# Dense stage of a split-float32 FFN: row tiles in pairs, 896 of 1160 columns by seven block products in place of eight

## The reference, cut to what matters

```
W = weights[condition]                        # one 64x64 matrix per batch, 16 in all
z = einsum('bct,bcd->bdt', x, W)              # mixes the 64 channels of a batch
result = einsum('bnd,od->bno', z, W_base) + b_base
probs  = softmax(einsum('bnd,ed->bne', z, W_gate))          # 8 experts
top_p, top_i = top_k(probs, 2); top_p /= sum(top_p)
h = einsum('bnd,erd->bner', z, A)             # 8 experts of rank 16
out = x + result + einsum('bner,eor->bno', h * route_w, B)
```

## Time and profile before

| | |
|---|---|
| median of 3 runs | 1025.07 us (1024.55 to 1025.69) |
| span of the profiled execution, first to last instruction | 1023.8 us |
| TensorE (PE) busy | 1015.4 us, 5834 matmuls |
| VectorE busy | 372.2 us |
| ScalarE busy | 209.5 us |
| GpSimd busy | 339.2 us |
| DMA | 107.09 MB, mean 105 GB/s |

### The profile page before, as it was taken

The page is one execution under the profiler, slowest core; times in us unless marked ns, Lnnn a source line. Parts: engine busy times, 40 slices in busy tenths (PEclk is TensorE's granted clock), DMA queues, the critical chain, the costliest instruction groups (busy, mean ns, idle before and its releaser), DMA issues.

```text
span 1023.8 us, 17244 instructions
## 1 busy us (share of the span) xinstructions
PE 1015.4 (99%) x5834; PEld 1007.7 (98%) x5834; DVE 372.2 (36%) x1240; ACT 209.5 (20%) x470; POOL 339.2 (33%) x264
## 2 busy tenths in 40 slices
PE   8999999999999999999999999999999999999998
PEld 6999999999999999999999999999999999999998
DVE  6533333333333333333333333333333333333334
ACT  6211211211122112111221221112212212122121
POOL 1424334233243342432423424324234243242331
PEclk9999999999999999999999999999999999999999
DMA  9323132232231322322213223223132232222311
GB/s 306 147 104 119 68 121 95 90 123 82 102 122 62 123 91 94 123 82 102 112 73 123 88 96 123 82 102 115 69 123 86 99 123 82 102 105 79 123 66 57
DMA packets 32009, 107.09 MB, mean 105 GB/s; under 512 B 3457, under 2 KB 6914, under 8 KB 32002
## 3 DMA queue, kind: packets, MB, share of 16 engines
q1 hardware_dynamic: 32000, 107.00, 28.5%
q10 hardware_dynamic: 2, 0.00, 0.0%
HBM read 73.43 MB, written 33.55 MB: 105 GB/s over the span
## 4 chain that ended last, share of the span: by engine, by line
PE 97%; DVE 1%; DMA 1%; SPq 1%; ACT 0%; issue 0%; DVEq 0%
PE ps_z L521 77%; PE ps_out L533 10%; PE ps_out L548 9%; DMA table_raw<-in_cond_w 1%; PE ps_hwt L541 1%; SPq L221 1%; DVE w_lo L421 0%; DVE w L462 0%; SPq L224 0%; DVE z_lo L431 0%; DVE table L484 0%; ACT table L376 0%; DVE o_sb L444 0%; SPq L234 0%; DVE pick L466 0%
## 5 line engine op out<-in xcount | busy, mean ns | idle before, releaser
L521 PE MATMUL ps_z<-w_hi,x_hi 128*128 128x384 f32 (+1 forms) x1536 | 526.0, 342 | 1.5 <-DVE w_lo L421 1.4
L521 PE MATMUL ps_z<-w_hi,x_lo 128*128 128x384 f32 (+1 forms) x1536 | 519.7, 338 | 0.0
L521 PE MATMUL ps_z<-w_lo,x_hi 128*128 128x384 f32 (+1 forms) x1536 | 519.5, 338 | 0.0
L306 POOL TENSOR_TENSOR x_lo<-xt_sb,x_hi 128x1024 fp32r<-128x1024 f32 x62 | 149.2, 2407 | 550.7 <-ACT x_hi L353 550.7
L521 PEld LDWEIGHTS ps_z<-w_hi,x_hi 128*128 128x128 f32 x1536 | 288.5, 188 | 5.7 <-DVE w_lo L421 1.9
L521 PEld LDWEIGHTS ps_z<-w_lo,x_hi 128*128 128x128 f32 x1536 | 288.7, 188 | 0.0
L521 PEld LDWEIGHTS ps_z<-w_hi,x_lo 128*128 128x128 f32 x1536 | 288.7, 188 | 0.0
L431 DVE TENSOR_TENSOR z_lo<-ps_z,z_hi 128x384 fp32r<-128x384 f32 (+1 forms) x192 | 107.6, 560 | 485.6 <-ACT z_hi L357 485.6
L357 ACT CAST z_hi<-ps_z 128x384 fp32r<-128x384 f32 (+1 forms) x192 | 92.4, 481 | 613.2 <-PE ps_z L521 612.3
L311 POOL TENSOR_TENSOR o_sb<-o_sb,bias 128x1024 f32<-128x1024 f32 x64 | 153.4, 2397 | 2.0 <-DMA o_sb<-in_x 2.0
L533 PE MATMUL ps_out<-z_hi,mix 128*128 128x384 f32 (+1 forms) x384 | 129.6, 337 | 1.1 <-POOL mix L299 0.8
(11 more groups left out here) (41 smaller groups left out, 362.0 us busy)
## 6 DMA issues: line engine op xcount, KB each, us to landing
o_sb<-in_x SPq DMA_DIRECT2D x64, 512.0 KB, 3.3
out_x<-o_sb SPq DMA_DIRECT2D x63, 512.0 KB, 2.6
xt_sb<-in_x_t SPq DMA_DIRECT2D x62, 512.0 KB, 4.4
w_raw<-in_w_t SPq DMA_DIRECT2D x8, 384.0 KB, 9.0
w_raw<-in_w_t SPq DMA_DIRECT2D x8, 196.0 KB, 4.9
xt_sb<-in_x_t SPq DMA_DIRECT2D x4, 256.0 KB, 4.8
table_raw<-in_cond_w SPq DMA_DIRECT2D x2, 256.0 KB, 8.7
b_raw<-in_b_t SPq DMA_DIRECT2D x1, 512.0 KB, 11.8
```

Source lines behind the costliest of these rows:

```text
L306: pool.tensor_tensor(x_lo[slot][:], xt_sb[slot][:], x_hi[slot][:].bitcast(F32), ALU.subtract).then_inc(s_x_lo, 1)
L521: mm = pe.matmul(z_bank(i, c)[:, 0:width[c]], a[slot][:, k, :], w[:, k, cols(c)], start=(k == 0 and q == 0), stop=(k == KT - 1 and q == 2))
```

## The change

Row tiles are worked in pairs (tile 2p is t = 0, tile 2p+1 is t = 1). The weight columns are cut anew: L is 312 base columns with the 136 of A and the gate (448), Q is 448 base columns, R is 264 base columns. Over L and Q the pair is a 2x2 block product: the rows are the two tiles, the inner axis has two halves of 4 blocks k, the columns are L and Q. It is done by Strassen's seven products in Winograd's form (`strassen`, 12 matmuls of 448 columns each) in place of eight, R stays plain (`plain_r`, 12 matmuls of 264 columns each, four times). Four blocks of x (`A11`, `A12`, `A21`, `A22`, 512 elements in a partition) are loaded into `raw`; four sums of them, S1 to S4, are made on GpSimd, four sums of weights, T1 to T4, once on VectorE. S4 is written in place over `raw[A12]`, the lo part of S1, S2 and S3 in place over the sum. The products accumulate in the banks `ps_1`, `ps_6` and `ps_5`: `u2` = P1 + P6, `u3` = u2 + P7, and VectorE's `add` brings a copy of P1 and earlier sums together out of them. The first pair is plain, while the weights arrive and T1 to T4 are made. The stores of the last pair go out in six parts.

How many instructions of each kind a pair has, before and after, is this:

| per pair | before | after |
|---|---|---|
| dense matmuls | 144 (48 of 392, 96 of 384 columns) | 132 (84 of 448, 48 of 264) |
| mix matmuls | 18 | 18 (12 of 448, 6 of 264) |
| lora matmuls | 18 | 18 (6 each of 312, 448, 264) |
| transposes | 2 | 2 |
| GpSimd passes over 512 elements | 0 | 12 (4 blocks' lo, 4 sums, 4 sums' lo) |
| GpSimd passes over 1024 elements | 4 | 2 |
| ScalarE passes over 512 elements | 0 | 8 (and none of the 2 over 1024) |
| VectorE adds of banks | 0 | 5 |

The diff, cut to the loop of each engine:

```diff
-BASE_COLS = [256, 384, 384]
+BASE_COLS = [312, 448, 264]
...
+            def load_raw(p, j):
+                tile, half = 2 * p + j // 2, j % 2
+                src = x_t[tile] if isinstance(tile, int) else \
+                    x_t[bass.ds(tile, 1)].rearrange("a p k r -> (a p) k r")
+                sp.dma_start(raw[j][:], src[:, half * KH:(half + 1) * KH, :]).then_inc(s_raw_in[j], 16)
...
+            def store(p, t):
+                sp.wait_ge(s_out[t][(Q, R)[t]], p + 1)
+                sp.dma_start(out[bass.ds((2 * p + t) * P, P), :], o_sb[t][:]).then_inc(s_stored[t], 16)
...
+            def step(p, last):
+                sp.wait_ge(s_stored[0], 16 * p)
+                load_x(p, 0)
+                if not last:
+                    sp.wait_ge(s_a_lo[A21], p + 1)
+                    load_raw(p + 1, A21)
+                    sp.wait_ge(s_a_lo[A22], p + 1)
+                    load_raw(p + 1, A22)
+                    sp.wait_ge(s_s_sum[3], p)
+                    load_raw(p + 1, A11)
+                    sp.wait_ge(s_s_lo[4], p)
+                    load_raw(p + 1, A12)
+                store(p - 1, 1)
+                sp.wait_ge(s_stored[1], 16 * p)
+                load_x(p, 1)
+                if not last:
+                    store(p, 0)
+            pairs(sp, step)
...
+            def sum_s1(p):
+                pool.wait_ge(s_raw_in[A21], 16 * p + 16)
+                pool.wait_ge(s_raw_in[A22], 16 * p + 16)
+                pool.wait_ge(s_p[5], p)
+                pool.tensor_tensor(s1[:], raw[A21][:], raw[A22][:], ALU.add).then_inc(s_s_sum[1], 1)
+            def sum_s2(p):
+                pool.wait_ge(s_s_sum[1], p)
+                pool.wait_ge(s_p[3], p)
+                pool.tensor_tensor(s2[:], s1[:], raw[A11][:],
+                                   ALU.subtract).then_inc(s_s_sum[2], 1)
+            def sum_s3(p):
+                pool.wait_ge(s_p[7], p)
+                pool.tensor_tensor(s3[:], raw[A11][:], raw[A21][:], ALU.subtract).then_inc(s_s_sum[3], 1)
+            def sum_s4(p):
+                pool.wait_ge(s_s_sum[2], p)
+                pool.wait_ge(s_a_lo[A12], p + 1)
+                pool.tensor_tensor(raw[A12][:], raw[A12][:], s2[:], ALU.subtract).then_inc(s_s_sum[4], 1)
...
+            def step(p, last):
+                sum_s2(p)
+                a_rest(p, A12)
+                sum_s4(p)
+                s_rest(p, 2, s2[:], s2_hi, s2_lo)
+                sum_s3(p)
+                s_rest(p, 3, s3[:], s3_hi, s3_lo)
+                s_rest(p, 1, s1[:], s1_hi, s1_lo)
+                a_rest(p, A22)
+                a_rest(p, A21)
+                pool.wait_ge(s_mixed[0][Q], p)
+                fetch_mix(p, 0)
+                pool.wait_ge(s_mixed[1][R], p)
+                fetch_mix(p, 1)
+                s_rest(p, 4, raw[A12][:], s2_hi, s2_lo)
+                residual(p, 0)
+                if not last:
+                    a_rest(p + 1, A11)
+                residual(p, 1)
+                if not last:
+                    sum_s1(p + 1)
...
+            def s_top(p, j, whole, hi):
+                act.wait_ge(s_s_sum[j], p)
+                act.copy(hi[:], whole).then_inc(s_s_hi[j], 1)
...
+            def added_top(p, t, c):
+                act.wait_ge(s_z_sum[t, c], p)
+                z_top(t, c, z_sum[t][:, cols(c)])
...
+            def step(p, last):
+                act.wait_ge(s_p[1], p + 1)
+                act.copy(z_sum[1][:, cols(L)], ps_1[:, 0:NS]).then_inc(s_p1_out, 1)
+                hwt_top(2 * p - 1)
+                act.wait_ge(s_p[6], p + 1)
+                s_top(p, 4, raw[A12][:], s2_hi)
+                act.wait_ge(s_p[2], p + 1)
+                z_top(0, L, ps_1[:, 0:NS])
+                s_top(p, 1, s1[:], s1_hi)
+                act.wait_ge(s_r_sum[0], p + 1)
+                z_top(0, R, ps_r[:, 0:width[R]])
+                if not last:
+                    a_top(p + 1, A11)
+                    a_top(p + 1, A12)
+                exps(2 * p)
+                added_top(p, 1, Q)
+                added_top(p, 1, L)
+                hwt_top(2 * p)
+                added_top(p, 0, Q)
+                if not last:
+                    s_top(p + 1, 2, s2[:], s2_hi)
+                exps(2 * p + 1)
+                act.wait_ge(s_r_sum[1], p + 1)
+                z_top(1, R, ps_r[:, 0:width[R]])
+                if not last:
+                    a_top(p + 1, A21)
+                    a_top(p + 1, A22)
+                    s_top(p + 1, 3, s3[:], s3_hi)
...
+            def added_rest(p, t, c):
+                z_rest(p, t, c, z_sum[t][:, cols(c)])
+            def add(bank, other, to):
+                return dve.tensor_tensor(to, bank[:, 0:NS], other, ALU.add)
...
+            def step(p, last):
+                dve.wait_ge(s_p1_out, p)
+                dve.wait_ge(s_p[6], p + 1)
+                add(ps_6, p1, u2).then_inc(s_u2, 1)
+                hwt_rest(2 * p - 1)
+                output(p - 1, 1, L)
+                z_rest(p, 0, L, ps_1[:, 0:NS])
+                output(p - 1, 1, Q)
+                output(p - 1, 1, R)
+                z_rest(p, 0, R, ps_r[:, 0:width[R]])
+                gate(p, 0)
+                dve.wait_ge(s_p[7], p + 1)
+                add(ps_6, p1, u3).then_inc(s_u3, 1)
+                dve.wait_ge(s_p[5], p + 1)
+                dve.wait_ge(s_u3, p)
+                add(ps_5, u3, u3).then_inc(s_z_sum[1, Q], 1)
+                added_rest(p, 1, Q)
+                dve.wait_ge(s_p[4], p + 1)
+                add(ps_6, p1, p1).then_inc(s_z_sum[1, L], 1)
+                hwt_rest(2 * p)
+                added_rest(p, 1, L)
+                dve.wait_ge(s_p[3], p + 1)
+                dve.wait_ge(s_u2, p)
+                add(ps_5, u2, u2).then_inc(s_z_sum[0, Q], 1)
+                output(p, 0, L)
+                added_rest(p, 0, Q)
+                output(p, 0, R)
+                gate(p, 1)
+                z_rest(p, 1, R, ps_r[:, 0:width[R]])
+                output(p, 0, Q)
...
+            def product(bank, hi, lo, u_hi, u_lo, opens, closes, goes_on=False):
+                for k in range(KH):
+                    for q, (a, w) in enumerate(((hi, u_hi), (hi, u_lo), (lo, u_hi))):
+                        mm = pe.matmul(bank[:, 0:w.shape[-1]], a[:, k, :], w[:, k, :],
+                                       start=(opens and k == 0 and q == 0),
+                                       stop=(closes and k == KH - 1 and q == 2), skip_group_check=goes_on)
+                return mm
+            def strassen(bank, hi, lo, g, opens):
+                return product(bank, hi, lo, w_hi[:, g], w_lo[:, g], opens, True, goes_on=not opens)
...
+            def step(p, last):
+                pe.wait_ge(s_a_lo[A11], p + 1)
+                strassen(ps_1, a_hi[A11], a_lo[A11], B11, True).then_inc(s_p[1], 1)
+                pe.wait_ge(s_out[0][Q], p)
+                mix_chunk(p - 1, 1, Q)
+                pe.wait_ge(s_out[0][R], p)
+                mix_chunk(p - 1, 1, R)
+                pe.wait_ge(s_t_lo[2], 1)
+                pe.wait_ge(s_s_lo[2], p)
+                strassen(ps_6, s2_hi, s2_lo, T2, True).then_inc(s_p[6], 1)
+                turn_hw(2 * p - 1)
+                pe.wait_ge(s_p1_out, p)
+                pe.wait_ge(s_a_lo[A12], p + 1)
+                strassen(ps_1, a_hi[A12], a_lo[A12], B21, False).then_inc(s_p[2], 1)
+                pe.wait_ge(s_hwt_lo, 2 * p)
+                lora(1, L)
+                lora(1, Q)
+                lora(1, R)
+                plain_r(ps_r, 0, 0, True, False)
+                plain_r(ps_r, 0, 1, False, True).then_inc(s_r_sum[0], 1)
+                pe.wait_ge(s_out[1][L], p)
+                mix_chunk(p, 0, L)
+                pe.wait_ge(s_t_lo[3], 1)
+                pe.wait_ge(s_s_lo[3], p)
+                pe.wait_ge(s_u2, p)
+                strassen(ps_6, s3_hi, s3_lo, T3, False).then_inc(s_p[7], 1)
+                pe.wait_ge(s_t_lo[1], 1)
+                pe.wait_ge(s_s_lo[1], p)
+                strassen(ps_5, s1_hi, s1_lo, T1, True).then_inc(s_p[5], 1)
+                pe.wait_ge(s_out[1][R], p)
+                mix_chunk(p, 0, R)
+                pe.wait_ge(s_t_lo[4], 1)
+                pe.wait_ge(s_a_lo[A22], p + 1)
+                pe.wait_ge(s_u3, p)
+                strassen(ps_6, a_hi[A22], a_lo[A22], NT4, False).then_inc(s_p[4], 1)
+                turn_hw(2 * p)
+                pe.wait_ge(s_s_lo[4], p)
+                pe.wait_ge(s_z_sum[1, Q], p)
+                strassen(ps_5, s2_hi, s2_lo, B22, False).then_inc(s_p[3], 1)
+                pe.wait_ge(s_hwt_lo, 2 * p + 1)
+                lora(0, L)
+                lora(0, R)
+                pe.wait_ge(s_a_lo[A21], p + 1)
+                plain_r(ps_r, 1, 0, True, False)
+                pe.wait_ge(s_out[0][L], p + 1)
+                mix_chunk(p, 1, L)
+                plain_r(ps_r, 1, 1, False, True).then_inc(s_r_sum[1], 1)
+                pe.wait_ge(s_out[1][Q], p)
+                mix_chunk(p, 0, Q)
```

(49 more changed lines are left out.)

603 lines of the change are left out of this document (300 added, 303 removed).

## The result

The changed kernel took 1206.05 us, the median of four runs (1205.79 to 1211.13), against 1024.84 us, the median of four, for the kernel before on the same chip: a ratio of 1.1778, 95% interval 1.1757 to 1.1799. The forecast was 1185 us, slower; the range 1045 to 1295. The profiled execution was the slowest of the four, 1211.13 us; its span of 1209.0 us lies 2.95 us above the median.

What follows compares the result with a forecast made beforehand. TensorE, 99% busy, was taken to bound the kernel before; afterwards a ring of in-order waits. 15.8 + 31.5 + 30 x 36.5 + 34.0 + 8 = 1184.3 of span, plus 1.3 for the median: 1185 us, range 1045 to 1295.

Steps and rivals of the forecast that it cites:

- Step 2: GpSimd's list from S1's lo to S4's lo at 10.2 us; first mix fetch ends at 7.1, TensorE idle 2.8 us.
- Step 5: TensorE from P4 round to the next P2: five products 12.2 us, the rest 6.7, together 18.9 us.
- rival D: TensorE's clock halves after the 3.65 us idle, doubling P4: 2.4 us a pair, 1257 us; after both idles 1330; chance 0.13.
- the forecast's signs: Expected in the profile: 170 matmuls a pair, TensorE some 80% busy, period 36.5 us, P4 and mix waits, clock 1.00.
- Contention, 1.0 on the path: VectorE's remainders and gates meet GpSimd passes and each engine waits for the other: 1.0 us a pair, bounds 0 and 4.
- rival C: VectorE-GpSimd contention decides if A12 lands at 4.8 us, gates running into passes: 4 us more a pair, 1305 us; chance 0.11.
- Rival B: A12-to-exponential link absent or covered, only mix late on TensorE: 31.8 us a pair, 1045 us; chance 0.08.
- the link through A12: A12's load after S4's lo, then ScalarE's cast ahead of the exponential, delays gate, u3 and P4: TensorE idle 3.65 us.
- the late reload of x: x for residual(p,1) lands at 17 us; S2's lo ends about 26, P6 wants S2 at 30.5, so hidden.
- the first ring: From P2 through GpSimd, A12's load, ScalarE and gate to P4, then TensorE back to P2: 16.6 + 18.9 = 35.5 us.
- Rival A: All waits hidden, TensorE's work alone counts: 29.0 us a pair, 956 us in total; chance 0.07.
- The ends: Opening and last pair outside the loop: opening 5 us above its 31.5 of matmuls, last pair 34.0, bare tail 3 more.

Runs made afterwards that it cites:

- the best order: Changed kernel with GpSimd's list filled, mix Q and R behind P6 and the exponential ahead of the casts: 970.59 us, ratio 0.9478 to the kernel before.

## Why the prediction was right, point by point

The direction, the mechanism and its place held; the total was 21 us (1.8%) low. That it came so near is partly luck, since two errors of a pair nearly cancelled. By its steps, counted from the end of P2 at 509.32:

| step | forecast | measured |
|---|---|---|
| TensorE's pace, 448 / 264 columns | 0.203 / 0.121 | 0.205 / 0.122 |
| GpSimd pass over 512 | 1.22 | 1.24 from start to start (511.89 to 514.36 for two) |
| S1's lo begins | 1.4 | 1.33 |
| mix ready, TensorE idle | 7.1, 2.8 | 5.94, 1.6 |
| S4's lo ends | 10.2 | 9.03 |
| load of A12 | 3.0 | 2.98 (518.50 to about 521.5) |
| exponential to hw | 2.04 | 2.03 |
| P4 starts, TensorE idle | 16.6, 3.65 | 15.42, 3.5 |
| P4 to the end of P2 | 18.9 + 1.0 | 21.67 |
| period | 36.5 | 37.09 here, 37.08 mean |
| ends | 89.3 | 1209.0 - 1112.4 = 96.6 |

**Step 2, the fetch**, was too dear by 1.2 us. The forecast carried over 0.90 us ahead of the first cast from the earlier trace rows; in the new list the cast at 514.36 follows A21's lo with no gap. The likely reason is that the register load is read while the passes before it run, where the kernel before had in front a wait for the end of its residual pass; no run takes that apart.

**Step 5 and rival D, the clock.** The forecast put the clock outside the sum, at 0.13, as 2.4 us a pair for the whole of P4. It fell in 25 of the 30 pairs, and cost less than that where it fell: in the pair of the table P4 to the transpose took 3.58 us and the transpose to the lora 3.05, against 2.44 and 2.55, so 1.64; keeping TensorE busy gave back 1.35 in the mean. This term is the one that was mis-sized, from nothing to about 1.4, and a clock of 1.00 among the forecast's signs was wrong with it. The fetch's error hid most of it: -1.2 + 1.6 and small ones make +0.58. The kernel before had no idle stretch that could show it. The Trainium skill, TensorE: Matmul & The Clock Gate, section HAM oscillation — how this bites in real kernels, describes gaps in a matmul stream that send the clock to half rate again and again; the trace agrees for 25 pairs of 30 (0.50 from 526 to 527 us), and in the other 5 the clock held.

**Contention, 1.0 on the path,** was right in sum: mix Q waits 0.92 (539.38 to 540.30), behind the gate(p,1) that the passes stretch. VectorE's timeline of the kernel after:

```profile
535.18 0.90 DVE L563 CAST top_atf<-top_at 128x2 f32<-128x2 uint32 x1
...
536.17 1.16 DVE L568 TENSOR_SCALAR w<-e,e_inv 128x2 f32<-128x2 f32 x1
537.44 1.33 DVE L572 TENSOR_SCALAR pick<-expert,top_atf,w 128x8 f32<-128x8 f32 x2
```

These take 0.17, 0.23 and 0.48 us in gate(p,0) of the same pair (516.88 to 523.46), where no pass is beside them. This is the second half of rival C, gate(p,1) among GpSimd's passes; its condition did not come, since A12 landed 2.98 us after its issue.

**Rival B was mispriced.** It said that without the link through A12 the period would be 31.8. With the exponential moved it was 36.6. Two things were left out: gate(p,0) would move beside GpSimd's passes, and exps(2p+1) stands behind the next S2 on ScalarE. The forecast had seen the late reload of x and followed it to P6 only, not to the gate. So it knew the first ring and not how close the second was.

**Rival A was right about the size of the saving,** 956 us if all is hidden: the best order reaches 970.6, and the 2.5 us a pair that seven products save are 2.2 in its period (31.5 - 29.3).

**The ends** cost 7 us more than forecast. The opening was put at 5 us above its matmuls; there alone TensorE waits 4.3 us for mix and 6.4 for an output of VectorE, the longest of both kinds in the waits view above. The output stands behind gate(0,1), which takes 6.1 us from its exponential to hw. GpSimd's passes hold the gate before it too: the cast of top_atf takes 2.27 us, as the timeline of the kernel after shows. How the 7 us part between opening and last pair was not taken apart.

```profile
32.21 2.27 DVE L563 CAST top_atf<-top_at 128x2 f32<-128x2 uint32 x1
```

## What to carry to other kernels

An engine at 57% can still set the time: in a list that runs in order, count the longest ring through the lists and not the busy shares, and put a pass that must wait behind those that need not. When one ring is cut, price the next before expecting its whole gain; here the second lay 0.4 us under the first. A row of short VectorE instructions beside GpSimd's passes is priced at up to one pass for each of them. A stall of some microseconds on TensorE costs more than itself, since the matmuls behind it may run at half the clock.

## What was not expected of the hardware

The clock falls sooner than I had thought, and not every time. With the exponential moved, the first matmul of P4 after an idle of 1.85 us ran at half rate, and in the next pair one after 1.87 us did not. In the timeline of that kernel the second matmul of the one P4 and the first of the other read:

```profile
516.76 0.57 PE L663 MATMUL ps<-w_lo,a_hi 128*128 128x448 f32 x1
...
551.83 0.44 PE L663 MATMUL ps<-w_hi,a_hi 128*128 128x448 f32 x1 [1.87 <-DVE z_sum L536]
```

The periods of that kernel come in two kinds for it, 35.1 to 35.5 us and 36.8 to 37.4. In the kernel after the clock even held through an idle of 3.53 us. So the length of the idle stretch alone does not decide, and no run takes apart what else does.

And a held VectorE instruction waits for one GpSimd pass, not for the whole queue: in none of the twelve traces does an instruction of a gate take longer than the one pass of 1024 elements, 2.44 us at most, and the two picks of 3.48 us above ended one behind each pass. It is the next short instruction that meets the next pass. A longer one that gets in holds GpSimd in its turn, as the timeline of the kernel with GpSimd's list filled has it:

```profile
509.85 1.29 POOL L312 TENSOR_TENSOR s_sum<-raw 128x512 f32<-128x512 f32 x1
...
510.10 1.52 DVE L529 TENSOR_TENSOR z_lo<-z_sum,z_hi 128x448 fp32r<-128x448 f32 x1
511.21 1.56 POOL L317 TENSOR_TENSOR s_sum<-s_sum,raw 128x512 f32<-128x512 f32 x1
```

The VectorE instruction, 0.62 us long alone, waits for the end of the first pass and ends 0.48 us behind it, at 511.62; the second pass, begun meanwhile, takes 1.56 us and not 1.29.
